# A windowed-attention block: layer norm by whole groups with two buffers, inverse roots on VectorE, bias rows on GpSimd

## The reference

```python
h = _ln(x, ln1_g, ln1_b)                      # (x - mean) / sqrt(var + 1e-5) * g + b
h = jnp.roll(h, (-4, -4), axis=(1, 2))
win = _window_partition(h, 8)                 # windows of 64 tokens
q, k, v = jnp.split(win @ qkv_w + qkv_b, 3, axis=-1)       # 4 heads of 16
attn = einsum('bnhd,bmhd->bhnm', q, k) * 16 ** -0.5 + bias + mask
out = einsum('bhnm,bmhd->bnhd', softmax(attn), v) @ proj_w + proj_b
x = x + jnp.roll(_window_reverse(out), (4, 4), axis=(1, 2))
h2 = _ln(x, ln2_g, ln2_b)
return x + gelu(h2 @ fc1_w + fc1_b) @ fc2_w + fc2_b        # hidden width 256
```

## Time and profile before

| | |
|---|---|
| three runs | 516.34, 513.32, 516.05 us (median 516.05) |
| the profiled execution's own time (its span) | 516.1 us |
| PE busy | 462.7 us (90%) |
| PE weight loads | 352.7 us (68%) |
| DVE busy | 388.9 us (75%), 549 instructions |
| ACT busy | 359.0 us (70%) |
| POOL busy | 384.4 us (74%), 376 instructions |
| of POOL: L367, adding the maximum | 123.9 us in 64 |
| of POOL: L333, power -0.5 | 105.0 us in 62 |

### The profile page before, as it was taken

One profiled execution on the slowest core, in us unless ns is written; L12 is line 12 of the kernel. 1 busy time (PEld: TensorE's weight loads), 2 busy tenths in 40 slices (PEclk: granted clock), 3 DMA queues, 4 the chain that ended last, 5 costly groups with the idle time before them and its releaser, 6 DMA issues.

```text
span 516.1 us, 21507 instructions
## 1 busy us (share of the span) xinstructions
PE 462.7 (90%) x9630; PEld 352.7 (68%) x9630; DVE 388.9 (75%) x549; ACT 359.0 (70%) x501; POOL 384.4 (74%) x376
## 2 busy tenths in 40 slices
PE   0765799999899999999999999998799999999995
PEld 0533587787788788778788778677566666666664
DVE  2865688899779899879899899894467767666752
ACT  0236488878878878778778778775577777777761
POOL 2648959879969979969969978942288888888830
PEclk9998799999999999999999999999999999999999
DMA  8201424411411411411011011000003303311333
GB/s 162 60 1 31 99 47 96 114 34 25 104 38 30 104 39 28 102 34 37 23 29 40 23 25 41 24 23 3 3 3 84 84 12 74 84 46 40 83 83 83
DMA packets 9986, 27.04 MB, mean 52 GB/s; under 512 B 3368, under 2 KB 3368, under 8 KB 7976
## 3 DMA queue, kind: packets, MB, share of 16 engines
q1 hardware_dynamic: 9896, 25.68, 21.1%
HBM read 9.15 MB, written 8.39 MB: 34 GB/s over the span
## 4 chain that ended last, share of the span: by engine, by line
PE 53%; DVE 17%; POOL 16%; ACT 8%; issue 2%; DMA 2%; SPq 0%; ACTq 0%; DVEq 0%
PE work L693 20%; PE outs L693 10%; POOL probs L367 9%; PE trans L693 8%; PE scores L693 6%; DVE negmax L482 5%; DVE probs L476 4%; POOL stat_rstd L333 4%; PE scores L829 3%; PE trans L789 3%; DVE x L517 3%; DMA params<-in_params 2%; POOL xn L344 2%; DVE x L533 2%; ACT qT L605 2%
## 5 line engine op out<-in xcount | busy, mean ns | idle before, releaser
L367 POOL TENSOR_TENSOR probs<-probs,negmax 128x1024 f32<-128x1024 f32 x64 | 123.9, 1937 | 38.4 <-DVE negmax L482 38.4
L333 POOL TENSOR_TENSOR stat_rstd<-stat_var,minus_half 128x8 f32<-128x8 f32 (+1 forms) x62 | 105.0, 1693 | 5.0
L476 DVE TENSOR_TENSOR probs<-scores,bias 128x1024 f32<-128x1024 f32 x64 | 77.9, 1218 | 32.9 <-PE scores L693 32.9
L638 ACT ACTIVATE probs<-probs 128x1024 f32<-128x1024 f32 x64 | 67.7, 1058 | 50.3 <-POOL probs L367 49.8
L338 POOL TENSOR_TENSOR xn<-x,stat_mean 128x256 f32<-128x256 f32 (+1 forms) x91 | 77.2, 867 | 4.1
L482 DVE TENSOR_REDUCE negmax<-probs 128x16 f32<-128x1024 f32 x64 | 78.1, 1220 | 2.2
L693 PEld LDWEIGHTS work<-params,probs 128*64 128x64 f32 x2048 | 62.2, 138 | 23.5 <-DVE x L570 20.5
L693 PE MATMUL scores<-kX,qT 32*64 32x128 f32 x2048 | 71.5, 276 | 7.2 <-DVE probs L476 4.6
L693 PE MATMUL outs<-vX,probsT 128*64 128x34 f32 x2048 | 72.9, 226 | 5.1 <-ACT probsT L643 4.1
L693 PEld LDWEIGHTS outs<-vX,probsT 128*64 128x64 f32 x2048 | 66.0, 139 | 16.4 <-issue 9.5
L789 PEld LDWEIGHTS trans<-ident,probs 128*128 128x128 f32 x512 | 56.2, 142 | 26.4 <-issue 14.2
(11 more groups left out here) (64 smaller groups left out, 691.7 us busy)
## 6 DMA issues: line engine op xcount, KB each, us to landing
kX<-kT SPq DMA_DIRECT2D x124, 64.0 KB, 2.0
x<-in_x SPq DMA_DIRECT2D x32, 224.0 KB
out<-x SPq DMA_DIRECT2D x28, 224.0 KB
x<-in_x SPq DMA_DIRECT2D x32, 32.0 KB
out<-x SPq DMA_DIRECT2D x28, 32.0 KB
out<-x SPq DMA_DIRECT2D x16, 56.0 KB
params<-in_params SPq DMA_DIRECT2D x1, 741.5 KB, 12.3
out<-x SPq DMA_DIRECT2D x16, 8.0 KB
```

The source lines that it names most:

```text
L333: nc.gpsimd.tensor_tensor(stat_rstd[:, cols], stat_var[:, cols], minus_half[:, cols], ALU.pow).then_inc(ln_rstd, pieces)
L367: nc.gpsimd.tensor_tensor(e, e, top, ALU.add).then_inc(shifted, 1)
L476: nc.vector.tensor_tensor(e[:, :].rearrange("q (u a m) -> q a u m", u=2, a=2), scores[:, :].rearrange("q (a u m) -> q a u m", a=2, u=2), b ...
L638: nc.scalar.activation(probs[n % 4][:, :], probs[n % 4][:, :], ACT.Exp)\
```

## The change

The layer norm goes by whole groups. Its steps are spread over two groups of attention ahead of use, with two buffers `xn` and two buffers `stat_rstd`. In the MLP the norm of four pieces is done as one group as well, from the table `LN_LATE`; the first two of its eight groups are done in the attention loop. The power on POOL is gone. In its place `root(G)` on DVE works on the 32 sums of squares per partition of a whole group at once: three small instructions make a first guess from the bits of the number, and three Newton turns of three instructions each refine it, each instruction waiting for the one before. The row biases `y_bias` and `bf2` are added by POOL, with the same shapes. One load of x is issued three steps earlier.

```diff
-LN_STEPS = {"sum": (-4, -4, -3, -2), "mean": (-4, None, -3, -2), "centre": (-4, -4, -3, -2),
-            "square": (-2, -1, 0, 1), "square_sum": (-1, 0, 1, 2), "rstd": (-1, 0, 1, 2),
-            "scale": (0, 1, 2, 3)}
+LN_STEPS = {"sum": (-18, -17, -16, -15), "mean": (-15,), "centre": (-14, -13, -12, -11),
+            "square": (-13, -12, -11, -10), "square_sum": (-12, -11, -10, -9), "root": (-9,),
+            "scale": (-8, -7, -6, -5)}
...
+LN_LATE = {"sum": (-2, -1, 0, 1), "mean": (1,), "centre": (2, 3, 3, 4), "square": (3, 3, 4, 4),
+           "square_sum": (3, 4, 4, 5), "root": (5,), "scale": (6, 7, 8, 9)}
+
+def ln_late_at(stage, s):
+    return [(GROUPS + m, i) for m in range(2, GROUPS) for i, at in enumerate(LN_LATE[stage])
+            if max(PIECES * (m - 2) + at, 0) == s]
...
-        xn = sb("xn", ROW)
+        xn = [sb(f"xn{i}", ROW) for i in range(2)]
...
-                if n in (1, STEPS - 2):
+                if n in (1, 3):
                     load(2 if n == 1 else 3)
... (POOL)
-                nc.gpsimd.tensor_tensor(stat_rstd[:, cols], stat_var[:, cols], minus_half[:, cols],
-                                        ALU.pow).then_inc(ln_rstd, pieces)
...
+            def add_y_bias(g, half):
+                pool.wait_ge(ln_centred, PIECES * (g + 1))
+                pool.wait_ge(y_bias_made, 1)
+                dst = as_tokens(x[:, g * ROW + half * 2 * PIECE:][:, 0:2 * PIECE])
+                nc.gpsimd.tensor_tensor(dst, dst, y_bias[:, :].unsqueeze(1).to_broadcast([P, 2 * WIN, C]),
+                                        ALU.add).then_inc(y_biased, 1)
+
+            def add_bf2(s):
+                pool.wait_ge(ln_centred, S + s + 1)
+                dst = as_tokens(x[:, s * PIECE:(s + 1) * PIECE])
+                nc.gpsimd.tensor_tensor(dst, dst, bf2[:, :].unsqueeze(1).to_broadcast([P, WIN, C]),
+                                        ALU.add).then_inc(bf2_added, 1)
...
             for n in range(PAIRS):
                 shift_pair(n)
                 norm(n)
-            for s in range(S - 2):
-                if s + 4 < S:
-                    centre2(s + 4)
-                if s + 3 >= PIECES and s + 3 < S:
-                    rstd(S + s + 3, (s + 3) % PIECES)
+                if n % STEPS in (3, 7):
+                    add_y_bias(n // STEPS, n % STEPS // 4)
+            for n in range(PAIRS, PAIRS + TAIL):
+                norm(n)
+            for s in range(S):
+                for group, _ in ln_late_at("mean", s):
+                    mean(group)
+                for group, i in ln_late_at("centre", s):
+                    centre_piece(group, i)
+                add_bf2(s)
... (DVE)
+            def root(G):
+                steps = iter(range(11 * G + 1, 11 * G + 12))
+                def then(done):
+                    k = next(steps)
+                    done.then_inc(ln_newton, 1)
+                    dve.wait_ge(ln_newton, k)
+                if G >= 2:
+                    dve.wait_ge(xn_ready, PIECES * (G - 1))
+                dve.wait_ge(ln_sq, PIECES * (G + 1))
+                then(nc.vector.tensor_scalar(stat_half[:, :], stat_sq[:, :], EPS, 0.5, ALU.add, ALU.mult))
+                then(nc.vector.tensor_scalar(stat_seed[:, :], stat_half[:, :].bitcast(I32), 1, None,
+                                             ALU.arith_shift_right))
+                then(nc.vector.tensor_scalar(stat_root[:, :].bitcast(I32), stat_seed[:, :], -1.0,
+                                             float(ROOT_SEED), ALU.mult, ALU.add))
+                for turn in range(3):
+                    last = turn == 2
+                    sign = -1.0 if last else 1.0
+                    then(nc.vector.scalar_tensor_tensor(stat_turn[:, :], stat_root[:, :], sign,
+                                                        stat_half[:, :], ALU.mult, ALU.mult))
+                    then(nc.vector.tensor_tensor(stat_turn[:, :], stat_turn[:, :], stat_root[:, :], ALU.mult))
+                    to = stat_rstd[G % 2] if last else stat_root
+                    done = nc.vector.scalar_tensor_tensor(to[:, :], stat_turn[:, :], 1.5 if last else -1.5,
+                                                          stat_root[:, :], ALU.add, ALU.mult)
...
-                if n < PAIRS and n % STEPS in (3, 5):
-                    add_y_bias(n // STEPS, (n % STEPS - 3) // 2)
... (DVE, the MLP's loop)
-                if s + 4 < S:
-                    sum2(s + 4)
-                if PIECES <= s + 2 < S:
-                    scale_rows(S + s + 2, (s + 2) % PIECES)
-                if PIECES <= s + 3 < S:
-                    square_sum(S + s + 3, (s + 3) % PIECES)
-                if s < S:
-                    dve.wait_ge(ln_centred, S + s + 1)
-                    dst = x[:, s * PIECE:(s + 1) * PIECE].rearrange("q (a f) -> q a f", f=C)
-                    nc.vector.tensor_tensor(dst, dst, bf2[:, :].unsqueeze(1).to_broadcast([P, WIN, C]),
-                                            ALU.add).then_inc(bf2_added, 1)
+                for group, i in ln_late_at("sum", s):
+                    sum_piece(group, i)
+                for group, i in ln_late_at("scale", s):
+                    scale_rows(group, i)
+                for group, i in ln_late_at("square_sum", s):
+                    square_sum(PIECES * group + i, i)
+                for group, _ in ln_late_at("root", s):
+                    root(group)
```

More of the change, by code:

```diff
@@ L98, in tasks_at @@
     return [task[1:] for task in TASKS if task[0] == n]
-LN_STEPS = {"sum": (-4, -4, -3, -2), "mean": (-4, None, -3, -2), "centre": (-4, -4, -3, -2),
-            "square": (-2, -1, 0, 1), "square_sum": (-1, 0, 1, 2), "rstd": (-1, 0, 1, 2),
-            "scale": (0, 1, 2, 3)}
-LN_STEPS_FIRST = {"sum": (-1,) * 4, "mean": (-1, None, -1, -1), "centre": (-1,) * 4,
-                  "square": (-1,) * 4, "square_sum": (0,) * 4, "rstd": (0, 0, 1, 1),
-                  "scale": (1, 1, 2, 2)}
+LN_STEPS = {"sum": (-18, -17, -16, -15), "mean": (-15,), "centre": (-14, -13, -12, -11),
+            "square": (-13, -12, -11, -10), "square_sum": (-12, -11, -10, -9), "root": (-9,),
+            "scale": (-8, -7, -6, -5)}
+LN_STEPS_EARLY = {
+    1: {"sum": (-1,) * 4, "mean": (-1,), "centre": (-1,) * 4, "square": (-1,) * 4,
+        "square_sum": (0,) * 4, "root": (0,), "scale": (1, 1, 2, 2)},
+    2: {"sum": (3, 3, 4, 4), "mean": (4,), "centre": (5, 5, 6, 6), "square": (6, 6, 7, 7),
+        "square_sum": (7, 7, 8, 8), "root": (8,), "scale": (8, 9, 10, 11)}}
+LN_AHEAD = GROUPS + 2
 def ln_at(stage, n):
     found = []
[L115 to L118, removed]
-    return found
+    for group in range(1, LN_AHEAD):
+        early = LN_STEPS_EARLY.get(group)
+        for i, at in enumerate((early or LN_STEPS)[stage]):
+            if n == (at if early else STEPS * group + at):
+                found.append((group, i))
+    return found
+LN_LATE = {"sum": (-2, -1, 0, 1), "mean": (1,), "centre": (2, 3, 3, 4), "square": (3, 3, 4, 4),
[3 more added lines that the diff above has]
+            if max(PIECES * (m - 2) + at, 0) == s]
 PARAM_COLUMNS = [("wqkv", 3 * P), ("gain", 2), ("shift", 2), ("bqkv", 3), ("turn", 2), ("bf1", 2), ("bproj", C),
@@ new lines, in centre_piece @@
+            def centre_piece(G, i):
+                if G < GROUPS:
+                    if G >= 2 and i == 0:
+                        pool.wait_ge(work_ready["XT"], COUNT["XT", G - 2, 1])
+                    for half in halves(G, i):
+                        done = centre(*half)
+                else:
+                    if G < GROUPS + 2:
+                        pool.wait_ge(work_ready["XT"], COUNT["XT", G - 2, 1])
+                    else:
+                        pool.wait_ge(xT2_ready, PIECES * (G - 2 - GROUPS) + i + 1)
+                    done = centre(as_tokens(xn[G % 2][:, i * PIECE:(i + 1) * PIECE]),
+                                  x[:, of_rows(G) + i * PIECE:][:, 0:PIECE], i * WIN, WIN)
+                done.then_inc(ln_centred, 1)
@@ L358, in _ @@
             centre(*first_half(0, 1)).then_inc(ln_centred, 1)
-            for j in (0, 2):
-                rstd(j + 1, j, 2)
             def shift_pair(n):
@@ L451, in _ @@
                 square_sum(j, j)
+            root(0)
             dve.wait_ge(y_bias_summed, 1)
@@ L686, in _ @@
                 gelu(s)
-                if PIECES <= s + 3 < S:
-                    square(S + s + 3, (s + 3) % PIECES, S + s + 4)
+                for group, j in ln_late_at("square", s):
+                    square(PIECES * group + j, j, PIECES * group + j + 1)
         @block.tensor
```

139 lines of the change are left out of this document (58 added, 81 removed).

## The result

The changed kernel takes 603.58 us (median of 4 runs, 601.72 to 603.91), the kernel before 516.19 on the same chip: a ratio of 1.1668, with a 95% interval of 1.1621 to 1.1715. The forecast was 550, its range ended at 566. The profiled span is 601.5 us, 85.4 more than before. TensorE's first product of fc1 divides it: it starts at 409.79 instead of 366.73 (+43.1), and from there to the end are 191.7 instead of 149.4 us (+42.3). Both stages lose about the same; the prediction had 11.4 and 22.7.

A forecast was written before the change was run, and what follows sets the result against it. PE was taken as the bound, busy throughout the MLP and 19.65 of 20 us in attention. From 516.1 us, -2 (first group), +22.7 (MLP roots) and +13.4 (attention roots) gave 550 us, range 510 to 566.

The forecast's parts named there:

- 22.7: MLP: roots taking turns with POOL's burst make PE stall at five pieces, 3.6, three times 4.3, and 6.2 us.
- The mechanism: DVE instructions with two SBUF inputs and POOL's wide additions alternate by whole instructions; in the MLP, 1.08 us per Newton instruction.
- Three of the twelve have one input and should pass freely: Root: its first three instructions do not wait for POOL; only the nine of the Newton turns do.
- The rule that stood beside it: Skill's rule: a two-port tensor_scalar may wait for POOL, so the root's first three would too; 6 us more, 556 us.
- Rival C: MLP: PE's clock falls in the stalls, 2.8 us more at each of five, 564 us; chance 0.08.
- It is 1.9 us late. Six roots give +11.4: Attention, steps 15 to 55: PE's next score starts 1.9 us late behind each of six roots, +11.4 us.
- The roots at steps 8 and 63: Attention: these two meet one square sum more, or the pipeline's end; estimated at +1 us each.
- 13.4: Attention: the root's whole cost, +11.4 us for six roots and +1 us each for two more.
- The earlier load cost nothing: Attention: the earlier load of x is free, lying 18 steps ahead of its use instead of 4.
- -2: First group: removing POOL's powers brings back 4.3 us less 2.4 us for a root, about 2 us.
- Rival A: Narrow DVE instructions do not take turns with POOL; MLP keeps 4.52 us an iteration, 521 us in all; chance 0.15.
- B: Rival: the root is cheap, 1.2 us, and POOL's relief decides; the V task's wait comes back, 508 us; chance 0.15.

The follow-up runs named there:

- e3: The changed kernel with DVE's root issued ahead of the row sum that releases POOL's burst in the MLP loop: 561.34 us.
- e9: The changed kernel with POOL's 128x512 additions in the MLP (centring and bias rows) each issued as two of 128x256: 583.29 us.
- e12: The changed kernel with the root's twelve instructions replaced by twelve dependent tensor_scalars of 128x32, inverse root left out: 601.94 us.
- e2: The changed kernel with the root's twelve instructions replaced by twelve dependent single-input sums (tensor_reduce) of the same width, inverse root left out: 547.74 us.
- e4: The changed kernel with dummy products on PE while it waits for the first piece of groups 2 to 6 in the MLP: 592.72 us.
- e11: The changed kernel with two dummy products on PE during its wait for the scores behind the root, at seven groups of the attention: 595.72 us.
- e1: The changed kernel with one tensor_scalar of 128x32 in place of the root's twelve instructions, inverse root left out: 529.28 us.
- e5: The changed kernel with only the load of group 2 moved, from step 1 to behind the first keys (step -1): 594.78 us.

## Why the prediction was wrong

- **The mechanism held.** DVE and POOL take turns by whole instructions, POOL's burst stands just ahead of the root, and PE waits for the scaling behind it (e3, e9). A bare instruction was taken as 0.2 us and is 0.22 with its gap.
- **"Three of the twelve have one input and should pass freely"** failed: they took 0.82, 0.97 and 1.20 us, and e12 shows that twelve of them cost as much as the whole root. The rows read for it were row sums, which are tensor_reduces and do pass (e2). The rule that stood beside it was right: in the MLP's longest wait all twelve took turns, not nine, and the root lasted 13.1 us instead of 10.3. Its 6 us in all were not measured by themselves. The other roots came to 9.4 us instead of 8.6 and the five waits to 29.9 instead of 22.7; POOL's bias rows, taken as 1.05, were 1.28.
- **Rival C, PE's clock, was dismissed at 0.08** by comparing busy shares with one window of the earlier trace rows in which the clock held. It was true, and not only in the MLP: 9.7 us there (e4), and some 1.3 us a group in the attention (e11), for which the prediction had no such case at all.
- **"It is 1.9 us late. Six roots give +11.4"** failed most. The first score was 2.6 us late, near the forecast. But the sum stopped there. PE then waits 0.86 us for the divide and goes on at the lower clock, so a group lost 4.7 to 5.3 us: 1.2 are there with a single tensor_scalar too (40.6 against 39.4 on average, e1), 3.8 are the root's, of them 2.57 the wait and 1.3 the clock (e11). The roots at steps 8 and 63, taken as +1 each, cost 2.5 and 4.0 us against e1; at 63 PE waits 4.12 us for the divide, 1.65 in e1. The root as a whole cost at least 33.8 us ahead of the MLP (e1), against 13.4. At step 7 it met POOL with its first instruction and not with its fourth, and the 128x1024 bias row took 2.37 us, not 1.94.
- **"The earlier load cost nothing"** failed by a load that the sum left out: group 2's is still issued at step 1 but summed at step 3, where the kernel before summed it at step 4. DVE waits 6.56 us for it, and e5 gets back 8.8 us. The 18 steps are the later groups'.
- **"-2" for the first group** was hidden by this load. With the load moved, steps 0 to 8 take 42.6 us (35.40 to 77.98), before 43.4 (35.92 to 79.34), although the root at step 0 costs 2.5 us there (9.95 us from step 0 to 1, 7.47 in e1). So what came back is 0.8 us, that root included.
- Rival A falls with e12, B with the 2.65 us of a bare root.

By runs, the 85.4 us are: 40.7 in the MLP and 33.8 ahead of it through the root, 9.2 ahead of it and 1.6 in the MLP left (e1). No run splits these 9.2: the wait for the load is in them (7.0 us in e1) and so are the 1.2 us a group.

## What to carry to other kernels

When an engine becomes late, follow the wait past its first victim: to the next wait that the same engine ends, and to TensorE's clock behind both. A chain of short dependent VectorE instructions is cheap where VectorE has time and GpSimd stands still, and costs one whole GpSimd instruction per link where it does not; look at what releases GpSimd's next burst, and put the chain ahead of it. A tensor_reduce passes where a tensor_scalar waits (e2, e12). When a run takes a part out, look whether what is left in its place still waits (e1).

## What the hardware showed that was not expected

- A VectorE tensor_scalar of 128x32 takes 0.18 us alone, mostly 0.8 to 1.2 beside GpSimd's 128x512 additions and 1.39 beside one of 128x1024; a tensor_reduce of the same size 0.185 to 0.189 throughout.
- 28 dummy products on TensorE, in waits of 29.9 us, shortened the MLP by 9.7 us (e4).
- GpSimd's addition of one bias row to all tokens is slower than its addition of one number per 64 columns (a mean, a maximum), at the same size: 2.37 against 1.90 us for 128x1024, 1.28 against 1.04 for 128x512.
